# The first batch's scan: GpSimd's addition of a state waits for the scan of the next state

## The reference, cut to what matters

```python
def step(h, t):
    delta_t, B_t, C_t, u_t = t
    dA = jnp.exp(delta_t[..., None] * A)
    h = dA * h + delta_t[..., None] * B_t[:, None, :] * u_t[..., None]
    y = jnp.einsum('bdn,bn->bd', h, C_t)
    return (h, y)
...
y = jnp.swapaxes(ys, 0, 1) + u * D_skip
y = y * jax.nn.silu(res)
return y @ out_proj_w.T
```

## Time and profile before

| what | value |
|---|---|
| runs of the kernel | 2493.75, 2499.45, 2513.72 us |
| median | 2499.45 us |
| the profiled execution, its own time | 2502.42 us |
| its span in the profile | 2500.5 us |
| around the span | 1.92 us |
| scan of batch 0 (first part 0 of DVE to the last part 2) | 70.3 to 163.5 us |
| mean granted TensorE clock | 0.909 of full speed |

### The profile page before, as it was taken

The page is one execution under the profiler, slowest core; times in us unless marked ns, Lnnn a source line. Parts: engine busy times, 40 slices in busy tenths (PEclk is TensorE's granted clock), DMA queues, the critical chain, the costliest instruction groups (busy, mean ns, idle before and its releaser), DMA issues.

```text
span 2500.5 us, 38952 instructions
## 1 busy us (share of the span) xinstructions
PE 2057.5 (82%) x11640; PEld 1430.8 (57%) x11640; DVE 1680.5 (67%) x2937; ACT 1187.7 (47%) x2702; POOL 951.3 (38%) x581
## 2 busy tenths in 40 slices
PE   4147788998899888998889878998889988989985
PEld 1013366665567556665566556665566655666764
DVE  2975678558965798558865788558876588645431
ACT  1214366345643466345653456344663456424631
POOL 0330366106920386106930277104850077203501
PEclk9558789999999999999999989998999998999997
DMA  2000002231123212231113212231123211142233
GB/s 103 0 0 17 17 35 71 91 109 43 57 70 113 69 51 74 90 110 40 61 64 119 68 42 84 67 106 56 43 68 116 85 45 55 65 133 71 71 105 116
DMA packets 82452, 175.06 MB, mean 70 GB/s; under 512 B 11448, under 2 KB 42560, under 8 KB 81984
## 3 DMA queue, kind: packets, MB, share of 16 engines
q1 hardware_dynamic: 78144, 164.05, 19.0%
q0 software_dynamic: 4096, 8.40, 1.1%
HBM read 123.71 MB, written 15.14 MB: 56 GB/s over the span
## 4 chain that ended last, share of the span: by engine, by line
PE 50%; DVE 22%; issue 14%; ACT 6%; POOL 4%; DMA 3%; SPq 1%; DVEq 0%; ACTq 0%; POOLq 0%
PE G L1065 7%; DVE HS L1542 7%; PE G L1050 5%; PE FM L1039 3%; PE FC L1027 3%; PE G L943 3%; PE G L954 3%; PE G L937 3%; ACT REG L1347 2%; DMA MW<-moe 2%; PE G L1082 2%; PE FM L907 2%; DVE maxes L1843 2%; DVE HC L1564 2%; PE FM L749 2%
## 5 line engine op out<-in xcount | busy, mean ns | idle before, releaser
L1542 DVE TENSOR_TENSOR_SCAN HS<-DA,D 128x1024 f32<-128x1024 f32 x128 | 374.8, 2928 | 20.5 <-ACT DA L1224 19.9
L1065 PEld LDWEIGHTS G<-REG 128*128 128x128 f32 x2560 | 350.4, 199 | 60.6 <-issue 50.2
L1065 PE MATMUL G<-REG 128*128 128x64 f32 x2560 | 358.6, 273 | 3.2 <-DVE REG L1855 3.2
L1967 POOL TENSOR_TENSOR Y<-Y,HC 128x1024 f32<-128x1024 f32 x114 | 269.1, 2361 | 181.3 <-DVE HC L1564 180.3
L1050 PE MATMUL G<-ident,REG 128*128 128x128 f32 x1280 | 242.1, 289 | 116.3 <-ACT REG L1347 114.0
L1347 ACT ACTIVATE REG<-G 128x128 f32<-128x128 f32 (+3 forms) x512 | 223.4, 436 | 121.4 <-PE G L1050 117.0
L1978 POOL TENSOR_TENSOR REG<-REG,cos_t 128x512 f32<-128x512 f32 x128 | 170.4, 1331 | 264.2 <-ACT REG L1323 264.1
L1050 PEld LDWEIGHTS G<-ident,REG 128*128 128x128 f32 x1280 | 149.0, 150 | 166.1 <-issue 132.6
L1339 ACT ACTIVATE REG<-G,maxes 128x128 f32<-128x128 f32 (+3 forms) x384 | 195.6, 510 | 81.9 <-DVE maxes L1843 81.9
L1981 POOL TENSOR_TENSOR REG<-REG 128x512 f32<-128x512 f32 x128 | 204.2, 1596 | 57.4 <-DMA REG<-ROT 48.8
L1039 PE MATMUL G<-REG 64*128 64x128 f32 (+3 forms) x768 | 217.8, 481 | 8.4 <-POOL REG L1981 7.4
(11 more groups left out here) (290 smaller groups left out, 4272.4 us busy)
## 6 DMA issues: line engine op xcount, KB each, us to landing
MW<-moe SPq DMA_DIRECT2D x120, 768.0 KB, 4.2
REG<-ROT SPq DMA_DIRECT2D x256, 128.0 KB
EW<-experts SPq DMA_DIRECT2D x16, 514.5 KB, 4.7
XG<-x_rows SPq DMA_DIRECT2D x8, 960.0 KB, 5.4
y_rows<-YO SPq DMA_DIRECT2D x120, 64.0 KB, 1.5
X<-xT SPq DMA_DIRECT2D x8, 256.0 KB, 6.1
W<-weights SPq DMA_DIRECT2D x1, 2048.0 KB, 9.5
REG<-xT SPq DMA_DIRECT2D x8, 256.0 KB, 3.2
```

Of the source, the lines that this page charges most:

```text
L1065: mm = pe.matmul(G[3][:, col:col + DK], PT[:, n % 2, c * P:(c + 1) * P], V[:, c, j * P + h * DK:j * P + (h + 1) * DK], start=c == 0, stop= ...
L1542: dve.tensor_tensor_scan(HS[:, :, :].rearrange("p h s -> p (h s)"), DA[:, n % 2, :, :].rearrange("p h s -> p (h s)"), D1[:, :, :].rearrang ...
L1967: pool.tensor_tensor(Y[:, :, :], Y[:, :, :], HC_EARLY if early else HC[:, n % 2, :, :], ALU.add).then_inc(y_add.sem, 1)
```

## The change

In `front` of GpSimd, the scan of batch 0, each addition but the last gets a wait in front of it: the addition of state n may start when n+2 scans of the batch are done, that is when the scan of state n+1 (counted from 0) has ended. The wait is carried by an increment of `pool_passed`. The addition of state 15 has no such wait. Nothing else is changed; `phase_1` and `phase_2`, with the scans of the batches 1 to 7, are as before.

```diff
@@ -2066,6 +2066,10 @@
                 front_du(b)
                 front_copy(b)
                 for n in range(STATES):
+                    if n + 1 < STATES:
+
+                        pool.wait_ge(scan_d.sem, scan_d.at(b, n + 2))
+                        pool.sem_inc(pool_passed, 1)
                     front_step(b, n)
                 front_end(b)
```

## The result

| | before | after |
|---|---|---|
| median of 19 runs each | 2499.45 us | 2485.2 us |
| lowest and highest | 2487.65, 2513.72 | 2474.7, 2497.55 |
| mean of the 19 | 2501.1 | 2485.6 |
| span of the profiled execution | 2500.5 | 2483.0 |
| first product by B of batch 0 to the output projection | 98.24 | 82.38 |

The ratio is 0.9938 with a 95% interval of 0.9918 to 0.9958: faster by 0.6%, clear of no change, and within the 1% band. The forecast was 2486.

The account below looks back on a forecast made before the run. DVE was taken to bound batch 0's scan stage. Scans 17.85 less 0.4 left overlap less 1.25 tail gave 16.2 us shorter (15.1 to 16.7), from 2502.3 to 2486 us; range 2476 to 2497, with rivals 2473 to 2502.

Parts of the forecast that it names:

- DVE bounds the stage and the addition lengthens the scan: Batch 0's scan: DVE busy 29.66 of 30 us; POOL's overlapping addition makes a scan 3.48 instead of 2.29 us.
- Rival 3: Batch 0's scans are long for another reason, such as ACT or PE; nothing gained, tail costs 1.25, 2503.7 us; chance 0.03.
- L: Delay from a scan's end to POOL's held addition in batch 0: taken as 0.22 us, bounds 0.14 and 0.30.
- rival 2: At the 15 added waits POOL wakes so late that additions overlap scans again; gain gone at 1.31 us; chance 0.04.
- Late by the overlap less 0.14 us: Rule for DVE scans starting while a POOL addition runs: delayed by the shared time less about 0.14 us.
- The scans: Batch 0: scans 1 to 15 each freed of 1.19, 17.85 us, less 0.4 us of overlap left in scans 2 to 15.
- The tail: Behind batch 0's last scan: last addition, multiplication by SR and output projection start 1.25 us later (1.17 to 1.33).
- Everything else is hidden: Batch 0: ACT's DA halves and PE's broadcasts keep up with periods of 4.70 instead of 5.89 us, at no cost.
- The level: Whole-kernel starting time for the forecast: 2502.3 us, the mean of four executions, giving 2486.
- What makes a run differ: Successive batches take 283.4 or 289.9 us, 6.5 apart, put down to PE's clock; the change redraws which lose it.

Follow-up runs that it names:

- e1: Kernel before, with only the first half of each addition in batch 0's scan; first product by B to output projection 81.00 us, single run 2483.65 us.
- e2: Changed kernel, each of the 15 waits on the next state's product by C instead of its scan; first product to projection 100.98 us, single run 2496.54 us.
- e3: Changed kernel, each of the 15 waits on the next state's product by B, so additions start inside a running scan; median 2473.31 us, ratio to before 0.990.
- e9: Changed kernel plus the same wait before the additions of states 3 to 14 of batches 1 to 7 in `phase_2`; median 2453.35 us, ratio to before 0.978.
- e7: Changed kernel plus a wait for the second scan before the first early state's addition of batches 1 to 7 in `phase_1`; single run 2492.91 us.
- e4: Changed kernel without the wait of the addition of state 14 alone; first product to projection 81.92 us, single run 2465.24 us.
- e5: Changed kernel with the scan wait on the addition itself and no semaphore increment; first product to projection 81.69 us, single run 2495.05 us.

## Why the prediction was right, point by point

- *DVE bounds the stage and the addition lengthens the scan.* Shown by e1 (shorter addition), e2 (later addition) and e3 (addition behind the scan's start). Rival 3 is out, and L of 0.24 puts rival 2 out.
- *Late by the overlap less 0.14 us.* After the change the addition ends at 82.71 + 2.36 = 85.07, 0.18 into the scan at 84.89, which is 0.04 longer. e1 gives 0.26 and 0.11, e2 1.42 and 1.28. Each time the difference is 0.14 or 0.15. The whole overlap, which the Trainium skill ("SBUF — State Buffer", section "Who interferes with whom") would charge, comes out too much: 14 x 0.18 = 2.5 us against the 0.57 measured. Whether POOL lets go before its recorded end or the scan can do without for its first 0.14 us is not told by these runs.
- *L.* Taken as 0.22 between 0.14 and 0.30, measured 0.24. So 0.04 was left of a scan's delay instead of 0.03.
- *The scans.* Forecast 17.85 - 0.4 = 17.45 us less, measured 54.38 - 37.23 = 17.15. The 15 scans were longer by 17.72 us in all, not 17.85 (1.19 was the first of them, the others are 1.18), and 0.57 was left instead of 0.4.
- *The tail.* Forecast 1.25, measured 2.67 - 1.40 = 1.27. The front is 15.86 us shorter, forecast 16.2.
- *Everything else is hidden.* ACT and PE kept up with 4.76 us a state; all scans after the second take 2.32 to 2.34, and none of DVE's products starts late.
- *The level.* The forecast of 2486 lies within 1 us of the median and the mean of the changed kernel, and part of that is luck: the level of 2502.3 was taken from four executions and is 1.2 above the mean of 19, while the gain of 16.2 is 0.7 above the difference of the means, so that the two errors cancel in part. The two means of 19 are 15.5 us apart, so the front's gain arrived whole within their uncertainty (standard deviations of 6.7 and 7.3 us give a standard error of 2.3 on the difference). Of the profiled executions' 17.5 us, 15.9 are the front, 0.85 an earlier start of it, and the rest is what is left of larger differences in later batches that cancel: 2.5 and 3.6 more, 6.9 less.
- *What makes a run differ.* Here a step failed, though it moved no number: the prediction put the batches' 6.5 us down to the clock. By the timelines the clock only sets it off; some 6 us of it are the same stall that the change removes from batch 0, in another place, and in e9 the batches with the low clock are as short as the others. The prediction said that "the scans and POOL's work then fall in another order" and did not ask what held the scans of 4.9 to 5.6 us.

## What to carry to other kernels

When an instruction's duration is bimodal and its size is not, lay the other engines' timelines beside it: an engine that the instruction doesn't wait for by a semaphore can still hold it. Between DVE instructions with two sources in SBUF and POOL's operations, the start decides who pays, so let POOL start beside instructions that read PSUM, or just after the long one has begun; a microsecond too late and the gain is gone. Look at what POOL does just before, too: behind an indirect DMA without a gap the addition got ahead of a scan that had started 0.64 us earlier. Count what the held operation meets at its new place, small instructions on the critical chain above all, and look at every place that has the symptom, not only at the one that is easiest to reason about, each by itself: the wait paid in the later states and cost 1.5 us a batch in the early one.

## What the runs showed of the hardware

- The addition blocks not only scans. A DVE `tensor_scalar` on 128x4 int32 with its source and result in SBUF took 1.96 us instead of 0.17 while an addition ran (e7), where products with one source in PSUM on 128x1024 are untouched (1.21 to 1.22).
- A scan that starts under an addition ends as if the way were free 0.13 to 0.15 us before the addition's recorded end (overlaps of 0.18 to 1.42 us).
- Two POOL operations without a gap keep DVE out for both (5.32 us for a scan of 2.28); a gap of 0.16 us between them is enough for DVE to get in (583.48 to 589.21 in the changed kernel), and so is one of 0.08 (e4, 141.34 to 141.41).
- The issue of an indirect DMA on POOL took 3.73 us instead of 0.96 where a scan started 0.7 us into it (L1992, 871.86 in the changed kernel), but 0.96 where one started 0.33 us into it (L2017, 931.42 in e9). What tells the two apart is open.
- An increment between a wait and POOL's operation costs 0.09 us (e5), the waits behind it included.
